# A chain of graph networks on one core: three root products and the first weight splits placed among the sort's permutation batches, the input loaded in five parts

## The chip, the core and the metric

The kernel runs on one core of a Trainium2 chip. The time is the device time of one execution in microseconds (us). The engines are named as in the profile: PE is TensorE, DVE VectorE, ACT ScalarE, POOL GpSimd, SP SyncE. PEld is PE's weight load, which overlaps the matrix products. Every engine has a sequencer of its own that works its instructions off in program order and tells the others of progress through semaphores.

## The reference

The input is x with 625 nodes of 768 features and a list of 10,000 edges (src, dst, one of four types). Four graph networks follow on one another, each with a residual and a layer norm: a relational network of three layers, a two-layer graph convolution, and two attention networks. Only the first layer of the first one matters here:

```python
def _rgcn_conv(x, weight, root, bias, src, dst, etype):
    n = x.shape[0]
    out = x @ root + bias
    for r in range(NUM_REL):
        sel = etype == r
        self_f = sel.astype(x.dtype)
        deg = jnp.zeros((n,), x.dtype).at[dst].add(self_f)
        norm = jnp.where(sel, 1.0 / jnp.maximum(deg[dst], 1.0), 0.0)
        h_r = x @ weight[r]
        msgs = h_r[src] * norm[:, None]
        out = out + jax.ops.segment_sum(msgs, dst, num_segments=n)
    return out
```

## The kernel before

The graph is turned into four dense 625 x 625 matrices of edge counts, one for each relation, so that all sums over edges become matrix products. Building them is the first tenth of the program and the only part that the change touches. It has these steps.

**Front.** SP loads the edges (L749), then x as one transfer (`x_nat`, L750), the bias (L751) and the first five weight chunks (L758). DVE and POOL work out from the edges a place for each of them in an order by source and destination block.

**Sort.** Ten batches of 1,000 edges each. For a batch DVE makes one-hot matrices (`fill`, L1585 to L1593, four instructions, two buffers), and PE multiplies them (`permute`, L2475, eight products of 176 columns that all add into PSUM bank 0). Operand elements of these products lie eight fp16 elements apart (`[:, :, c]` with `BATCH` = 8). Among the batches x is transposed, one block of 125 nodes at a time: PE transposes (`turn`, six instructions, L2399), ACT rounds the result to `xT_hi` (L1021), DVE makes the remainder `xT_lo` (`lower`, L1532). The transposes use banks 5, 6 and 7 in turn. Weights are split in the same way: ACT makes `w_hi` (L1076), DVE `w_lo` (`weights`, L1656).

**Sweeps.** Three sweeps of 44 tiles. A tile holds 128 sorted edges. DVE makes a one-hot of the destination for each tile (L1632), and in the first two sweeps one of the source (L1630; ACT makes 27 of these 88, L1087 and L1092). PE adds their product into the banks (`tile_sums`, L2550): one product of 512 columns and one of 114, whose place in PSUM is worked out from a register at run time. Ten destination one-hots fit in the ring `onehot_dst`, so DVE may be ten tiles ahead. After a sweep ACT reads the banks.

**Root products.** x @ root is computed as ten pieces (two halves of the columns times five node blocks; `early`, L2499 to L2505). A piece is 18 products of 384 columns, accumulated in bank 7; ACT copies it out (L1057). Two of the pieces also load registers for the tiles to come. All ten stand in the sweeps: four after tiles 8, 17, 26 and 35 of the first, three after tiles 14, 24 and 34 of the second, one after tile 12 of the third and one after each of the first two sweeps.

The order is written out once, in `adjacency_plan`; PE, ACT and DVE each walk this list and take the steps that are theirs:

```python
for b in range(BATCHES):
    out += [("fill", b), ("perms", b)]
    if 0 <= b - 2 < NB:
        out.append(("turn", b - 2))
    if 0 <= b - 4 < NB:
        out.append(("lower", b - 4))
out += [("weights", 0, RAW), ("sorted",)]
```

SP loads a further weight chunk only when DVE has made `w_lo` of the chunk five before it. The functions, as the profile numbers their lines:

## Time and profile before

| | |
|---|---|
| median of 3 runs | 1485.93 us (1485.71 to 1486.21) |
| the profiled execution's own time | 1481.86 us |
| its span, first to last instruction | 1480.0 us |
| PE busy | 1385.7 us, 94% of the span |
| DVE, ACT, POOL busy | 53%, 29%, 37% |
| mean granted PE clock | 0.972 |

Times within the profile count from the first instruction. "Granted clock" is the share of 2.4 GHz that PE was given; it has two levels, 1.2 and 2.4 GHz (0.50 and 1.00). Where the profile holds no record of it the column reads 1.00. A product's duration in the profile includes the time until its result has left the array, so products in a row overlap; the distance from start to start is what one costs. "Idle before" names who ended an engine's wait; "issue" means that no semaphore of another engine did.

### The profile page before, as it was taken

Reading aid. Unit: us, or ns where it says so; the run is one execution under the profiler, and the core shown is the slowest. Engines: PE = TensorE matmul, PEld = TensorE weight load, DVE = VectorE, ACT = ScalarE, POOL = GpSimd, SP = SyncE. Lnnn points to the kernel's source line nnn. Section 1 sums busy time; section 2 is a strip of 40 time slices with the busy share of each in tenths; the row PEclk is TensorE's granted clock in tenths of the full one; section 3 lists DMA queues with packets and bytes.
Section 4 is the critical chain, followed back from the end, with each engine's and each line's share of the span. In section 5 each row is a group of like instructions: output and inputs, shape, how many; then the busy total and the mean of one; then the engine's idle time right before and its main releaser. Section 6 shows DMA issues by size and latency. Waiting matters only on the chain.

```text
span 1480.0 us, 22384 instructions
## 1 busy us (share of the span) xinstructions
PE 1385.7 (94%) x7674; PEld 1285.4 (87%) x7674; DVE 779.1 (53%) x1856; ACT 433.8 (29%) x932; POOL 543.5 (37%) x617
## 2 busy tenths in 40 slices
PE   5999999999999999999999899889988999788797
PEld 3677999999999999999999889889978977677784
DVE  7876755134444365662223443545464614599644
ACT  2555421101100011110111221244574334445431
POOL 8001243242425344343433342044335545345530
PEclk9999999999999999999999999999999999967899
DMA  3111111122343152341212121122102211200001
GB/s 114 54 31 36 33 42 55 33 64 65 99 131 114 38 149 60 102 134 49 65 35 63 54 64 33 39 81 77 33 22 75 75 43 38 75 1 1 1 11 53
DMA packets 57781, 86.46 MB, mean 58 GB/s; under 512 B 6447, under 2 KB 54438, under 8 KB 57563
## 3 DMA queue, kind: packets, MB, share of 16 engines
q1 hardware_dynamic: 45184, 65.82, 15.1%
q10 hardware_dynamic: 12504, 19.36, 4.3%
q8 instruction: 63, 1.03, 0.3%
q14 instruction: 30, 0.25, 0.1%
HBM read 83.24 MB, written 1.92 MB: 58 GB/s over the span
## 4 chain that ended last, share of the span: by engine, by line
PE 76%; DVE 13%; ACT 3%; POOL 3%; issue 3%; DMA 2%; DVEq 0%; ACTq 0%; SPq 0%; POOLq 0%
PE psum L2410 13%; PE psum L2414 13%; PE psum L2413 13%; PE psum L2427 8%; PE psum L2430 8%; PE psum L2888 4%; PE psum L2550 3%; DVE max_scratch L2115 2%; PE psum L2475 2%; POOL w_lo L904 2%; PE psum L2789 1%; PE psum L2793 1%; PE psum L2794 1%; PE psum L2938 1%; PE psum L2399 1%
## 5 line engine op out<-in xcount | busy, mean ns | idle before, releaser
L2410 PE MATMUL psum<-w_lo,xT_hi 128*125 128x384 f32 (+5 forms) x1140 | 390.3, 342 | 7.1 <-DVE x_nat L1843 2.6
L2414 PE MATMUL psum<-w_hi,xT_hi 128*125 128x384 f32 (+5 forms) x1140 | 385.7, 338 | 0.0
L2413 PE MATMUL psum<-w_hi,xT_lo 128*125 128x384 f32 (+5 forms) x1140 | 385.6, 338 | 0.0
L891 POOL CAST w_hi<-w_raw 128x384 fp32r<-128x384 f32 x190 | 104.4, 549 | 590.0 <-PE psum L2414 483.2
L2410 PEld LDWEIGHTS psum<-w_lo,xT_hi 128*125 128x125 f32 (+1 forms) x1140 | 213.4, 187 | 10.5 <-POOL w_lo L904 3.4
L1685 DVE TENSOR_TENSOR h_lo<-psum,h_hi 125x384 fp32r<-125x384 f32 (+1 forms) x120 | 67.0, 558 | 286.2 <-ACT h_hi L1064 284.9
L1064 ACT ACTIVATE h_hi<-psum 125x384 fp32r<-125x384 f32 (+1 forms) x120 | 59.1, 492 | 532.1 <-PE psum L2414 527.7
L2413 PEld LDWEIGHTS psum<-w_hi,xT_lo 128*125 128x125 f32 (+1 forms) x1140 | 213.9, 188 | 0.4
L2414 PEld LDWEIGHTS psum<-w_hi,xT_hi 128*125 128x125 f32 (+1 forms) x1140 | 213.4, 187 | 0.0
L893 POOL TENSOR_TENSOR w_lo<-w_raw,w_hi 128x384 fp32r<-128x384 f32 x190 | 200.9, 1058 | 15.2
L2427 PE MATMUL psum<-h_lo,adjacency 125*125 125x384 f32 (+3 forms) x600 | 203.5, 339 | 2.1 <-issue 1.9
L2430 PE MATMUL psum<-h_hi,adjacency 125*125 125x384 f32 (+3 forms) x600 | 202.8, 338 | 0.0
L904 POOL TENSOR_TENSOR w_lo<-w_raw,w_hi 128x384 fp32r<-128x384 f32 x86 | 88.9, 1066 | 108.6 <-ACT w_hi L1248 108.6
L2427 PEld LDWEIGHTS psum<-h_lo,adjacency 125*125 125x125 f32 (+1 forms) x600 | 111.4, 186 | 3.3 <-issue 2.7
L2430 PEld LDWEIGHTS psum<-h_hi,adjacency 125*125 125x125 f32 (+1 forms) x600 | 111.7, 186 | 0.0
L2888 PE MATMUL psum<-features,score_tiles 125*125 125x257 f32 (+2 forms) x380 | 106.3, 430 | 0.0
L2888 PEld LDWEIGHTS psum<-features,score_tiles 125*125 125x125 f32 x380 | 69.8, 187 | 27.4
L1868 DVE CUSTOM_DVE_ANT_0 score_products<-score_w_raw,score_a_rows 128x384 f32<-128x384 f32 (+2 forms) x116 | 58.1, 545 | 11.4 <-DMA score_w_raw<-weights_dram 7.9
L1829 DVE SCALAR_TENSOR_TENSOR x_nat<-psum,inv_degrees,x_nat 125x384 f32<-125x384 f32 x100 | 54.3, 609 | 11.2 <-PE psum L2430 10.8
L2938 PE MATMUL psum<-features,more_tiles 125*125 125x97 f32 x240 | 40.9, 346 | 15.2 <-DVE more_tiles L2171 15.2
L2938 PEld LDWEIGHTS psum<-features,more_tiles 125*125 125x125 f32 x240 | 39.1, 259 | 18.2 <-issue 15.2
L1632 DVE TENSOR_SCALAR onehot_dst<-iota,dst_of_sweep 128x625 bf16<-128x625 f16 x132 | 46.5, 387 | 14.0 <-PE psum L2550 13.8
(342 smaller groups left out, 2209.8 us busy)
## 6 DMA issues: line engine op xcount, KB each, us to landing
w_raw<-weights_dram SPq DMA_DIRECT2D x296, 192.0 KB, 2.4
score_w_raw<-weights_dram ACTq DMA_DIRECT2D x58, 192.0 KB, 2.8
x_nat<-x_dram SPq DMA_DIRECT2D x1, 1875.0 KB
x_residual<-x_dram SPq DMA_DIRECT2D x1, 1875.0 KB
score_a_rows<-L_gnn_a_src_dram ACTq DMA_DIRECT2D x8, 192.0 KB, 3.5
score_a_rows<-L_gnn_a_dst_dram ACTq DMA_DIRECT2D x8, 192.0 KB, 4.8
out_dram<-x_residual SPq DMA_DIRECT2D x4, 375.0 KB
rgcn_bias<-rgcn_bias_dram SPq DMA_DIRECT2D x1, 1125.0 KB
```

Of the source, the lines that this page charges most:

```text
L891: nc.gpsimd.tensor_copy(mem.wh[:, slot, :], mem.raw[:, raw_slot, :]).then_inc(w_hi_ready, 1)
L893: nc.gpsimd.tensor_tensor(mem.wl[:, slot, :], mem.raw[:, raw_slot, :], mem.wh[:, slot, :].bitcast(F32), ALU.subtract).then_inc(w_lo_ready, 1)
L904: nc.gpsimd.tensor_tensor(mem.wl[:, c % WRING, :], mem.raw[:, c % RAW, :], mem.wh[:, c % WRING, :].bitcast(F32), ALU.subtract).then_inc(w_ ...
L1064: nc.scalar.activation(mem.hh[0:p, slot, 0:HW], bank(ring_bank(u), 0, HW, p), ACT.Copy).then_inc(h_hi_ready, 1)
L1685: nc.vector.tensor_tensor(o, p, h, ALU.subtract).then_inc(h_lo_ready, 1)
L2410: ins = nc.tensor.matmul(o, h, wl, start=(j == 0), stop=False, skip_group_check=True)
L2413: nc.tensor.matmul(o, l, wh, start=False, stop=False, skip_group_check=True)
L2414: ins = nc.tensor.matmul(o, h, wh, start=False, stop=stop and j == k - 1, skip_group_check=True)
L2427: ins = nc.tensor.matmul(o, a, mem.hl[0:p, slot, 0:width], start=(s == 0), stop=False, skip_group_check=True)
L2430: ins = nc.tensor.matmul(o, a, mem.hh[0:p, slot, 0:width], start=False, stop=(s == NB - 1), skip_group_check=True)
L2888: ins = nc.tensor.matmul(bank(q.out_bank(u), 0, width), p, feat_flat(q, k, a, a + width), start=(k == 0), stop=(k == NB - 1), skip_group_c ...
L2938: ins = nc.tensor.matmul(bank(Q2.out_bank(h), b * Q2.w, b * Q2.w + Q2.w), source_tile(Q2, h, k)[:, nodes(b)], feat_flat(Q2, k, h * Q2.w, h ...
```

## The change

The list becomes a fixed one. The transposes of blocks 0 and 1 stand ahead of the first batch, those of blocks 2, 3 and 4 after batches 1, 2 and 3; the remainders follow two batches earlier than before. They use banks 4, 5, 6 and 3 in turn. The first five chunks of weights are split in batches 2 and 3, the sixth in batch 4, chunks 6 to 9 on ACT from batch 5. The root pieces of blocks 0, 1 and 2 of the first half stand after batches 5, 7 and 8. The sweeps keep seven: after tiles 10 and 24 of the first, 14 and 30 of the second, 12 of the third, and one after each of the first two sweeps. x comes in five transfers, three from SP and two from ACT, and the bias is loaded after the first weight chunks.

```diff
-        ROOTS_AFTER = ((8, 17, 26, 35), (14, 24, 34), (12,))
+        ROOTS_AFTER = ((10, 24), (14, 30), (12,))
+        FIRST_TURNS = (4, 5, 6, 3)
...
-        WEIGHTS_AFTER = {(0, 4): (RAW, RAW + 1), (0, 27): (RAW + 1, WRING), (1, 10): (WRING, 12), (1, 25): (12, 15),
+        WEIGHTS_AFTER = {(0, 20): (RAW + 1, WRING), (0, 42): (WRING, 12), (1, 24): (12, 15),
                          (1, 40): (15, 16), (2, 27): (16, 2 * WRING)}
...
+            beside = {0: [("lower", 0)], 1: [("turn", 2), ("lower", 1)], 2: [("turn", 3), ("split", 0, RAW), ("lower", 2)],
+                      3: [("weights", 0, RAW), ("turn", 4), ("lower", 3)],
+                      4: [("split", RAW, RAW + 1), ("weights", RAW, RAW + 1), ("lower", 4)],
+                      5: [("root",) + roots.pop(0), ("split", RAW + 1, WRING)],
+                      7: [("root",) + roots.pop(0)], 8: [("root",) + roots.pop(0)]}
+            out += [("turn", 0), ("turn", 1)]
             for b in range(BATCHES):
-                out += [("fill", b), ("perms", b)]
-                if 0 <= b - 2 < NB:
-                    out.append(("turn", b - 2))
-                if 0 <= b - 4 < NB:
-                    out.append(("lower", b - 4))
-            out += [("weights", 0, RAW), ("sorted",)]
+                out += [("fill", b), ("perms", b)] + beside.get(b, [])
+            out.append(("sorted",))
...
-            sp.dma_start(mem.xn[0:BP, :, :], x.rearrange("(m p) d -> p m d", p=BP)).then_inc(x_loaded, 16)
...
+            for m in (0, 2, 4):
+                sp.dma_start(mem.xn[0:BP, m, :], x[m * BP:(m + 1) * BP, :]).then_inc(x_loaded[m], 16)
...
+            act.wait_ge(edges_loaded, 48)
+            for m in (1, 3):
+                act.dma_start(mem.xn[0:BP, m, :], x[m * BP:(m + 1) * BP, :]).then_inc(x_loaded[m], 16)
...
                 if step[0] == "turn":
-                    turn_hi(0, KC, mem.xh, ACT.Copy, step[1])
-                    if step[1] in (2, 4):
-                        first_split((step[1] - 2) // 2 * RAW, step[1] // 2 * RAW)
+                    turn_hi(0, KC, mem.xh, ACT.Copy, step[1], FIRST_TURNS)
+                elif step[0] == "split":
+                    first_split(*step[1:])
...
                 elif step[0] == "turn":
-                    if step[1] == 0:
-                        pe.wait_ge(x_loaded, 16)
-                    turn(KC, of(mem.xn), 0, step[1])
+                    pe.wait_ge(x_loaded[step[1]], 16)
+                    if step[1] == 1:
+                        pe.wait_ge(sizes_ready, 1)
+                    turn(KC, of(mem.xn), 0, step[1], FIRST_TURNS)
                 elif step[0] == "root":
-                    early(*step[1:], step[1:] in ((0, 1), (1, 1)))
+                    early(*step[1:], step[1:] in ((0, 3), (1, 1)))
```

## Rows read from the trace of the kernel before

**Rows 1.** Busy time by stretch (us), granted clock, DMA share

```profile
core 0: us, PE busy (x) PEld busy (x) DVE busy (x) ACT busy (x) POOL busy (x), PEclk, DMA share, GB/s
0.00:19.10 19.10, 2.88 (x23) 2.12 (x23) 11.75 (x37) 3.85 (x5) 16.27 (x45) 1.00 0.42 132
19.10:50.90 31.80, 31.73 (x110) 17.83 (x110) 25.68 (x52) 7.11 (x16) 16.06 (x30) 1.00 0.17 64
50.90:83.30 32.40, 31.79 (x166) 24.06 (x167) 28.10 (x109) 22.56 (x63) 0.00 (x0) 1.00 0.17 52
83.30:114.70 31.40, 30.63 (x170) 22.93 (x168) 24.76 (x79) 18.72 (x31) 0.00 (x0) 1.00 0.13 39
114.70:142.10 27.40, 24.55 (x133) 17.59 (x132) 18.42 (x51) 12.93 (x24) 2.22 (x2) 0.94 0.12 37
```

**Rows 2.** Chain that ended last, front and sort (start us, us, what)

```profile
18.14 0.95 DVE tile_onehot L1593 x2
19.13 7.83 PE psum L2475 x24
26.96 1.25 PE psum L2399 x6
28.21 2.52 PE psum L2475 x8
...
43.27 7.58 PE psum L2475 x24
```

**Rows 3.** Groups by form on PE: 26 to 48 us, then 340 to 360 us

```profile
L2475 PE MATMUL psum<-tile_onehot,slot_onehot 125*128 125x176 f16 x52 | 17.6, 497 | 0.0
L2399 PE MATMUL psum<-ident,x_nat 125*128 125x125 f32 x30 | 7.2, 411 | 0.0
...
L2399 PE MATMUL psum<-ident,x_nat 125*128 125x125 f32 x30 | 3.6, 272 | 0.4 <-DVE xT_lo L1530 0.4
```

**Rows 4.** Timeline of DVE, batches 4 to 6 and end of sort

```profile
34.53 0.53 DVE L1585 TENSOR_TENSOR same_tile<-iota_wide,tile_h 125x704 f16<-125x704 f16 x1 [0.81 <-PE psum L2475]
36.51 0.99 DVE L1532 TENSOR_TENSOR xT_lo<-psum,xT_hi 128x375 fp32r<-128x375 f32 x2
...
47.74 2.43 DVE L1656 TENSOR_TENSOR w_lo<-w_raw,w_hi 128x384 fp32r<-128x384 f32 x5
```

**Rows 5.** Timeline of ACT in the sort

```profile
35.16 1.11 ACT L1021 ACTIVATE xT_hi<-psum 128x375 fp32r<-128x375 f32 x2 [2.64 <-PE psum L2399]
36.16 2.17 ACT L1076 ACTIVATE w_hi<-w_raw 128x384 fp32r<-128x384 f32 x5
```

**Rows 6.** Timeline of PE: a root piece, tiles, a piece with register loads

```profile
58.94 0.42 PE L2499 MATMUL psum<-w_lo,xT_hi 128*125 128x384 f32 x1
...
62.17 2.63 PE L2550 MATMUL psum<-onehot_dst,onehot_src 128*125 128x512 bf16 x18
64.62 0.42 PE L2499 MATMUL psum<-w_lo,xT_hi 128*125 128x384 f32 x1
...
68.31 4.08 PE L2550 MATMUL psum<-onehot_dst,onehot_src 128*125 128x512 bf16 x17
```

**Rows 7.** Timeline of PEld (weight loads, two for each tile)

```profile
54.68 0.34 PEld L2550 LDWEIGHTS psum<-onehot_dst,onehot_src 128*125 128x125 bf16 x2 [0.20 <-issue]
55.21 0.34 PEld L2550 LDWEIGHTS psum<-onehot_dst,onehot_src 128*125 128x125 bf16 x2 [0.20 <-issue]
...
69.22 0.63 PEld L2550 LDWEIGHTS psum<-onehot_dst,onehot_src 128*125 128x125 bf16 x4 [0.18 <-issue]
70.04 0.26 PEld L2550 LDWEIGHTS psum<-onehot_dst,onehot_src 128*125 128x125 bf16 x2 [0.18 <-issue]
...
139.17 0.34 PEld L2550 LDWEIGHTS psum<-onehot_dst,onehot_src 128*125 128x125 bf16 x2 [0.20 <-issue]
139.70 0.34 PEld L2550 LDWEIGHTS psum<-onehot_dst,onehot_src 128*125 128x125 bf16 x2 [0.20 <-issue]
```

**Rows 8.** Waits by engine, 51 to 148 us (us in total, times, longest)

```profile
PEld psum L2550 <- issue: 15.2, 53, 1.5
DVE onehot_dst L1632 <- PE psum L2550: 13.8, 5, 4.9
```

**Rows 9.** Granted clock 0.50: stretches, and PE's timeline in the first

```profile
888.40:891.60 3.20, 3.20 (x12) 0.50 0.00 0
137.40:140.80 3.40, 3.40 (x14) 0.50 0.14 49
...
888.83 0.52 PE L2413 MATMUL psum<-w_hi,xT_lo 128*125 128x384 f32 x1
889.15 0.52 PE L2414 MATMUL psum<-w_hi,xT_hi 128*125 128x384 f32 x1
```

**Rows 10.** Timeline of SP's queue: issue of x

```profile
1.96 0.34 SPq L750 DMA_DIRECT2D x_nat<-x_dram  x1
```

More of the change, by code:

```diff
@@ L398, in program @@
         edges_loaded = sem("edges_loaded")
-        x_loaded = sem("x_loaded")
+        x_loaded = [sem(f"x_loaded{m}") for m in range(NB)]
         bias_loaded = sem("bias_loaded")
@@ L749, in _ @@
                 sp.dma_start(mem.edges_i[0:BP, i, :], v.rearrange("(p t) -> p t", t=ET)).then_inc(edges_loaded, 16)
-            sp.dma_start(mem.xn[0:BP, :, :], x.rearrange("(m p) d -> p m d", p=BP)).then_inc(x_loaded, 16)
-            sp.dma_start(mem.bias0[0:BP, :, :].rearrange("p l d -> p (l d)"),
-                         rgcn_bias.rearrange("(a l) d -> a (l d)", a=1).to_broadcast([BP, RLAYERS * D])
-                         ).then_inc(bias_loaded, 16)
+            for m in (0, 2, 4):
+                sp.dma_start(mem.xn[0:BP, m, :], x[m * BP:(m + 1) * BP, :]).then_inc(x_loaded[m], 16)
             def load(c, slot, first=False):
@@ L762, in _ @@
                 load(c, c, first=True)
+            sp.dma_start(mem.bias0[0:BP, :, :].rearrange("p l d -> p (l d)"),
+                         rgcn_bias.rearrange("(a l) d -> a (l d)", a=1).to_broadcast([BP, RLAYERS * D])
+                         ).then_inc(bias_loaded, 16)
             with sp.Fori(1, XRES_AT // RAW) as i:
@@ L1669, in _ @@
                 elif step[0] == "lower":
-                    turn_lo(0, KC, mem.xh, mem.xl, False, step[1])
+                    turn_lo(0, KC, mem.xh, mem.xl, False, step[1], FIRST_TURNS)
                 elif step[0] == "tile":
```

## The prediction, made before the result was known

> **What bounds the kernel now.** The page gives PE 94% of the span, so the first question is whether PE is limited by its array everywhere. The busy times by stretch [rows 1] split the touched part: front to 19.1 us, sort to 50.9, then three sweeps of 32.4, 31.4 and 27.4 us. The whole edit lives in these 142 us. PE does 2.9 us of work in the front and is "busy" for nearly all of the rest, but a busy share counts overlapping durations, so start-to-start distances decide.
>
> The chain of waits [rows 2] says that the front is DVE's (one-hots until 19.1) and the sort PE's: a batch of eight products takes 2.52 us, a block of transposes 1.25, and they follow without a gap. Ten batches and five blocks are 31.5 of the 31.7 us.
>
> Two things hide behind "PE". The first is the clock. The granted column reads 1.00 in the sort, yet six transposes take 1.25 us, with a duration of 411 ns each, where the same form later takes 272 [rows 3]. The first tiles after the sort start 0.53 us apart, exactly as at 139 us [rows 7], where the clock is recorded at 0.50 [rows 9]. So I read the sort and the first eight tiles as 1.2 GHz. Only after tile 8 does a tile cost 0.27: nine of them from 62.17 to 64.62 [rows 6].
>
> The second is PE's own instruction stream. After a plain root piece nine tiles take 2.45 us; after a piece that also loads registers, 68.31 onward, they take about 3.9 [rows 6], with 0.18 us gaps on PEld that nobody else ended [rows 7], 15.2 us of such gaps in all [rows 8]. Tile instructions work out addresses, and at 0.41 to 0.45 us a tile the sequencer is slower than the array. A plain root piece (18 products, 3.23 us) lets it run ahead, and the next nine tiles then go at the array's pace. A root piece in the sweeps thus costs 3.23 us and gives back about 1.5. The same pause lets DVE fill its ring; DVE waited 13.8 us for PE in the sweeps [rows 8].
>
> **The change, part by part.**
>
> *x in five transfers.* In the front x has from 1.96 us [rows 10] until 10.7 (end of PE's counting) to bring blocks 0 and 1. They are 0.77 MB; at the front's 132 GB/s [rows 1] that is 5.8 us, so they are there. Nothing on the chain waited for x before, so this is worth 0 by itself. The two issues on ACT stand ahead only of four clears needed at 50 us. The bias is needed after the sweeps: 0. The first weights are needed at about 30 us, behind 2.1 MB on SP's queue, or 16 us at that rate: 0.
>
> *Transposes 0 and 1 ahead of batch 0.* They lie in PE's idle time before 19.1: -2 x 1.25 = -2.5 us. If x were late they would delay batch 0 by as much as they miss; nothing in the rates says so.
>
> *Remainders and splits earlier, on DVE.* A fill takes about 2.0 us, a remainder 1.0, five w_lo 2.43 [rows 4]. Before, a batch with a transposition cost PE 3.77 and DVE 3.0, so DVE had 0.8 to spare, and the w_lo stood at the end beside batches 8 and 9, hidden. Now they stand in front of fill 4. I follow DVE: fill 0 ends 18.97, remainder 0, fill 1 ends 22.1, where PE was free at 21.6 (wait 0.5). Fills 2 and 3 are in time (29.4). Then DVE waits for ACT, whose five splits (2.17 us, [rows 5]) follow the rounding of block 3 and end at 32.5: w_lo done 33.1, remainder 3 at 34.1, fill 4 at 36.3. PE has finished batch 3 and transposition 4 at 33.4: wait 2.9. In the same way w_lo 5 and remainder 4 put fill 5 at 39.8 against 38.9: wait 0.9. Sum +4.3 us; bounds 0 (DVE catches up) and 4.3. I take 4.3.
>
> *Three root pieces into the sort.* PE has no gap there, so they lie on the path in full: 3.23 us each at the full clock, 18 x 0.32 = 5.76 at the slow one (889.15 - 888.83, [rows 9]), so 9.7 to 17.3 us. Dense products did raise the clock at 58.9, after the first tiles, while thirty microseconds of batches did not. So I expect each piece to begin slow and end fast and take the middle, 4.5 us: +13.5. ACT's copies and splits 6 to 9 run beside: 0.
>
> *What the batches after a root piece cost.* The trace has no batch at the full clock. Bounds: 2.52 us as now, or half, 1.26, for batches 6 to 9 (-5.0). A batch product takes 315 ns for 176 columns, where a plain product at the slow clock takes 320 for 384 [rows 2, 9]. It is limited by something other than the column rate, and I take it as unchanged: 0.
>
> The Trainium skill, "SBUF — State Buffer", section "Door 1: The DMA port swizzle", says that reads which enter a new 16-byte line each time pay a penalty. The operands here lie 16 bytes apart. The trace agrees that these products are slow (315 ns), not that the penalty ignores the clock. [...]
>
> *The sweeps without them.* Three plain pieces fewer: 3 x (3.23 - 1.5) = -5.2 us, plus one w_lo (0.5) that leaves DVE there: -5.7. Bounds: -9.7 if the tiles stay at 0.27 with no piece to run ahead in, and -4 if DVE, which needs 0.52 us for a tile with both one-hots, becomes the limit at the four w_lo now after tile 20. I take -5.7. The slow start of the sweeps stays: batch 9 and the wait for the sorted edges stand before it, as now.
>
> **Sum.** -2.5 + 4.3 + 13.5 = +15.3 in the sort (its end moves from 50.9 to about 66), -5.7 in the sweeps, net +9.6 us. On the profiled execution: 1481.86 + 9.6 = 1491.5. That one is 4.1 us below the median of the runs, so for the median I take 1485.93 + 9.6 = 1495.5 us.
>
> **Rivals.**
>
> *The clock rises and the batches follow it* (the other side). If the first root piece (5 us, starting slow) lifts the clock for good, pieces two and three take 3.23, and if batches scale with it, 6 to 9 take 1.26: sort +11.4 - 2.5 + 4.3 - 5.0 = +8.2. The sweeps then start at full clock and save the 1.2 us of bank starts too: -6.9. Net +1.3, 1487 us; if the tiles also kept 0.27, up to -3, 1483. It decides from the point where a batch takes under 1.6 us. For it: idle PE and slow clock vanish together. Against: 315 ns is not a column rate.
>
> *The clock stays up, the batches do not speed up.* Sort +11.4 + 1.8 = +13.2, sweeps -6.9: +6.3, 1492 us.
>
> *The slow clock holds throughout.* Each piece 5.76: sort +19.1, sweeps -5.7: +13.4, 1499 us.
>
> *The reorder does what it says.* PE's idle time in the sweeps is what the pieces leave, all 9.7 us come back, and DVE's waits in the sort do not appear: +13.5 - 2.5 - 9.7 = +1.3, 1487 us, and faster only with the cheaper batches (-3.7). Against: [rows 8] shows gaps that no root piece caused.
>
> **Numbers.** Forecast, slow-starting pieces with unchanged batches: 0.50. Clock up, batches unchanged: 0.14. Slow throughout: 0.10. Batches scale with the clock: 0.16, half of it within 3 us of before. Full return from the sweeps: 0.10. Range 1484 to 1500 us: from the scaling case with a little return, to slow throughout. The likeliest case's own range is 1491 to 1499. A measurement of this kernel tells about 0.2% (3 us) from no change. Slower: the first three, 0.74. The last two are split: same 0.14, faster 0.12.
>
> **What would show it.** Batch 0 still at 19.1 us, with twelve transposes before it. PE gaps before batches 1, 4 and 5. Root products 320 ns apart at the start of a piece and 176 at its end. Batches 6 to 9 at 2.52 us each. End of sort at 64 to 68. In the sweeps tiles at 0.44 after the pieces' lead is used up, and DVE's wait for PE well below 13.8 us. All after the sweeps is unchanged and shifted. The prediction is wrong above all if batches 6 to 9 are much shorter than 2.5 us, or if the three sweeps together lose over 9 us.

## The result, and the profile after

The changed kernel takes 1495.58 us (median of 4 runs, 1494.39 to 1496.47); the kernel before, run beside it, 1485.82 us (median of 4, 1483.34 to 1486.21). The ratio is 1.0065, 95% interval 1.0052 to 1.0079: slower by 9.8 us. 1495.5 was predicted.

The stretches of the changed kernel, and below them three shorter ones at one clock level. The sweeps are cut here where the bank products of each begin, some 3 us later than the inner cuts of [rows 1]:

```profile
core 0: us, PE busy (x) PEld busy (x) DVE busy (x) ACT busy (x) POOL busy (x), PEclk, DMA share, GB/s
0.00:19.10 19.10, 5.70 (x36) 4.30 (x36) 11.17 (x37) 5.79 (x9) 16.27 (x45) 1.00 0.44 136
19.10:64.90 45.80, 42.33 (x153) 27.50 (x153) 25.84 (x52) 8.51 (x19) 13.83 (x30) 0.96 0.18 61
64.90:97.00 32.10, 30.71 (x151) 21.17 (x151) 29.46 (x114) 24.45 (x68) 0.00 (x0) 0.89 0.13 38
97.00:127.20 30.20, 28.76 (x150) 20.00 (x151) 23.02 (x73) 16.18 (x24) 0.00 (x0) 1.00 0.09 27
127.20:152.00 24.80, 22.27 (x115) 15.08 (x116) 18.19 (x49) 9.87 (x18) 2.21 (x2) 0.86 0.14 41
46.70:51.50 4.80, 4.80 (x18) 2.26 (x17) 2.00 (x4) 2.14 (x5) 0.00 (x0) 1.00 0.00 0
65.70:72.50 6.80, 6.62 (x23) 3.58 (x22) 6.73 (x29) 4.94 (x16) 0.00 (x0) 0.50 0.01 2
144.20:151.00 6.80, 6.20 (x23) 3.78 (x24) 5.97 (x19) 0.00 (x0) 0.99 (x1) 0.50 0.22 68
```

The front is as long as before, and the sort lasts 45.8 us instead of 31.8. From bank products to bank products, the last to the product behind the last tile, the sweeps take 35.3, 31.3 and 24.1 us before and 32.0, 30.2 and 24.7 after. The last tile moves from 142.1 to 151.8 us, by 9.7, and the medians differ by 9.8: what happens until the last tile is the whole effect. (The two profiled executions differ by 14.2 us in their spans. The other 4.5 us lie behind the last tile, in work that the change does not touch, and are not in the medians.)

PE's timeline in the changed kernel. The transposes of block 1 waited for x, batches 1, 4 and 5 for DVE's one-hots, and the first root piece begins with products 0.32 us apart and ends with products 0.17 to 0.18 us apart:

```profile
10.51 1.49 PE L2406 MATMUL psum<-ident,x_nat 125*128 125x125 f32 x6
15.80 1.51 PE L2406 MATMUL psum<-ident,x_nat 125*128 125x125 f32 x6 [3.79 <-DMA x_nat<-x_dram]
19.09 2.74 PE L2482 MATMUL psum<-tile_onehot,slot_onehot 125*128 125x176 f16 x8 [1.78 <-DVE tile_onehot L1600]
22.18 2.74 PE L2482 MATMUL psum<-tile_onehot,slot_onehot 125*128 125x176 f16 x8 [0.35 <-DVE tile_onehot L1600]
...
36.27 2.74 PE L2482 MATMUL psum<-tile_onehot,slot_onehot 125*128 125x176 f16 x8 [2.56 <-DVE tile_onehot L1600]
39.56 2.74 PE L2482 MATMUL psum<-tile_onehot,slot_onehot 125*128 125x176 f16 x8 [0.55 <-DVE tile_onehot L1600]
41.86 0.77 PE L2506 MATMUL psum<-w_lo,xT_hi 128*125 128x384 f32 x1
42.42 0.53 PE L2511 MATMUL psum<-w_hi,xT_lo 128*125 128x384 f32 x1
42.74 0.53 PE L2512 MATMUL psum<-w_hi,xT_hi 128*125 128x384 f32 x1
...
46.31 0.34 PE L2511 MATMUL psum<-w_hi,xT_lo 128*125 128x384 f32 x1
46.49 0.33 PE L2512 MATMUL psum<-w_hi,xT_hi 128*125 128x384 f32 x1
...
46.67 5.27 PE L2482 MATMUL psum<-tile_onehot,slot_onehot 125*128 125x176 f16 x16
```

The last row is batches 6 and 7. They start at 46.67 and 49.23 us, 2.56 us apart, while the granted clock is 1.00 (the row 46.70:51.50 above): the higher clock gives a batch nothing. By starts, from batch to batch, the sort is now ten batches of 2.55 us, three blocks of transposes of 1.22, gaps of 0.54, 2.78 and 0.75 us before batches 1, 4 and 5, and pieces of 4.6, 4.7 and 3.2 us. A gap is some 0.2 us longer than the wait that the row shows.

DVE's timeline around the longest gap, with the wait for ACT's splits and the five `w_lo` ahead of fill 4:

```profile
28.89 0.51 DVE L1600 TENSOR_TENSOR tile_onehot<-same_tile,code_h 125x704 f16<-125x704 f16 x1
30.90 2.49 DVE L1663 TENSOR_TENSOR w_lo<-w_raw,w_hi 128x384 fp32r<-128x384 f32 x5 [1.50 <-ACT w_hi L1083]
33.32 0.99 DVE L1539 TENSOR_TENSOR xT_lo<-psum,xT_hi 128x375 fp32r<-128x375 f32 x2
34.23 0.51 DVE L1592 TENSOR_TENSOR same_tile<-iota_wide,tile_h 125x704 f16<-125x704 f16 x1
```

The waits after the sort (the totals of [rows 8]):

```profile
PEld psum L2557 <- issue: 19.5, 73, 1.6
DVE onehot_dst L1639 <- PE psum L2557: 10.1, 4, 3.4
```

With fewer pieces in the sweeps, PE's own instruction stream holds up the tiles 73 times instead of 53, 4.3 us more in all, and DVE waits 3.7 us less for room in its ring.

### The profile page after: what moved, and what is told of

The parts are those of the page before. It is cut to its first block, busy times and chain, and to the rows that moved or that the text cites. A ratio compares the mean times of both kernels' runs of the same rounds, so it can differ in the third digit from the quotient of the medians.

```text
span 1494.2 us, 22392 instructions
## 1 busy us (share of the span) xinstructions
PE 1398.4 (94%) x7674; PEld 1292.3 (86%) x7674; DVE 780.9 (52%) x1856; ACT 433.2 (29%) x932; POOL 540.9 (36%) x617
## 4 chain that ended last, share of the span: by engine, by line
PE 75%; DVE 14%; ACT 4%; POOL 3%; issue 2%; DMA 2%; DVEq 0%; ACTq 0%; SPq 0%; POOLq 0%
PE psum L2417 13%; PE psum L2421 13%; PE psum L2420 13%; PE psum L2434 8%; PE psum L2437 8%; PE psum L2896 5%; DVE max_scratch L2122 2%; PE psum L2946 2%; POOL w_lo L908 2%; PE psum L2557 1%; PE psum L2797 1%; PE psum L2801 1%; PE psum L2802 1%; PE psum L2482 1%; DVE onehot_dst L1639 1%
## 5 line engine op out<-in xcount | busy, mean ns | idle before, releaser
L1836 DVE SCALAR_TENSOR_TENSOR x_nat<-psum,inv_degrees,x_nat 125x384 f32<-125x384 f32 x100 | 54.3, 610 | 11.2 <-PE psum L2437 10.8
L2557 PE MATMUL psum<-onehot_dst,onehot_src 128*125 128x512 bf16 (+1 forms) x264 | 52.9, 336 | 4.2 <-DVE onehot_dst L1639 2.5
```

The lines of the kernel that those rows point to most:

```text
L2557: ins = nc.tensor.matmul(o, sources, mem.oh_dst[:, n % OH_RING, w:w + 512 if w == 0 else NC], start=False, stop=(t == GROUP - 1), skip_gro ...
```

## The experiments

The steps of the change were built up one by one, first on the kernel before (turns, splits), then with its root pieces moved elsewhere or cut. All stage times below are from one profiled execution of each; "last tile" is the start of PE's first product behind the last tile. Each ratio is against executions of the kernel before made beside that run (medians 1484.80 to 1486.12 us), so between rows made at different times the ratios are compared, not the medians.

| kernel | sort ends | last tile | against before | ratio, 95% interval |
|---|---|---|---|---|
| before | 50.7 | 142.1 | | |
| turns ahead | 49.5 | 140.2 | -1.9 | 0.9985 [0.9973, 0.9998] |
| and splits early | 52.3 | 143.5 | +1.4 | 1.0004 [0.9991, 1.0018] |
| and three pieces in the sort, cut short | 53.3 | 140.2 | -1.9 | 0.9988 [0.9977, 0.9999] |
| and these pieces whole: the change | 64.8 | 151.8 | +9.7 | 1.0065 [1.0052, 1.0079] |
| the change, its three pieces together | 64.9 | 151.5 | +9.4 | 1.0059 [1.0041, 1.0078] |

**Turns ahead alone.** x in five transfers and transposes 0 and 1 ahead of batch 0; splits, `w_lo` and root pieces as before.

```diff
+            beside = {0: [("lower", 0)], 1: [("turn", 2), ("lower", 1)], 2: [("turn", 3), ("lower", 2)],
+                      3: [("turn", 4), ("split", 0, RAW), ("lower", 3)], 4: [("split", RAW, WRING), ("lower", 4)]}
+            out += [("turn", 0), ("turn", 1)]
             for b in range(BATCHES):
...
             out += [("weights", 0, RAW), ("sorted",)]
```

> Of the change only the five transfers of x, the two transposed blocks ahead of batch 0 and the earlier remainders; weight splits and all ten root pieces stand as before the change. My theory: the two transpositions (1.25 us each) lie in PE's idle time before 19.1 us, one remainder ahead of fill 1 costs a wait of about 0.35 us, so the sort ends near 48.7 us instead of 50.9 and the time is 2.1 us below the kernel before. Rival: what is gained ahead of the sort is lost again in the sort or the sweeps, 0 us.

Measured: 1482.62 us, ratio 0.9985 [0.9973, 0.9998], 2.2 us less than the 1484.80 of the kernel before beside it. PE's timeline shows the one thing that was not as expected:

```profile
10.52 1.49 PE L2403 MATMUL psum<-ident,x_nat 125*128 125x125 f32 x6
16.16 1.51 PE L2403 MATMUL psum<-ident,x_nat 125*128 125x125 f32 x6 [4.15 <-DMA x_nat<-x_dram]
19.09 2.74 PE L2479 MATMUL psum<-tile_onehot,slot_onehot 125*128 125x176 f16 x8 [1.43 <-DVE tile_onehot L1597]
```

Block 1 of x, issued on ACT's queue, was there only at 16.2 us. It is still hidden, with 1.4 us to spare. The sort gets 1.2 us shorter: two turns of 1.22 fewer, and gaps of 0.54 and 0.73 before batches 1 and 5, where DVE comes late.

**Splits early as well.** The steps of the change on DVE and ACT, with the root pieces still in the sweeps.

```diff
-        WEIGHTS_AFTER = {(0, 4): (RAW, RAW + 1), (0, 27): (RAW + 1, WRING), (1, 10): (WRING, 12), (1, 25): (12, 15),
+        WEIGHTS_AFTER = {(0, 27): (RAW + 1, WRING), (1, 10): (WRING, 12), (1, 25): (12, 15),
...
-                      3: [("turn", 4), ("split", 0, RAW), ("lower", 3)], 4: [("split", RAW, WRING), ("lower", 4)]}
+                      3: [("weights", 0, RAW), ("turn", 4), ("lower", 3)],
+                      4: [("split", RAW, RAW + 1), ("weights", RAW, RAW + 1), ("lower", 4)],
+                      5: [("split", RAW + 1, WRING)]}
...
-            out += [("weights", 0, RAW), ("sorted",)]
+            out.append(("sorted",))
```

> The first experiment, and the weight splits moved into batches 2 to 5 as in the change; all ten root pieces stay in the sweeps. My theory: w_lo 0 to 5 ahead of fills 4 and 5 make PE wait 2.6 and 0.6 us, so the sort ends near 51.8 us, and one w_lo less in the sweeps gives back up to 0.5: 2.6 to 3.1 us above the first experiment, 0.5 to 1 us above the kernel before. Rival: DVE's spare time in the sort takes the splits up, same time as the first experiment.

Measured: 1486.24 us, ratio 1.0004 [0.9991, 1.0018], 3.6 us above turns ahead alone; the sort ends 2.8 us later and the last tile comes 3.3 us later. Batch 4 starts at 36.28 as in the changed kernel. DVE's waits are a cost of their own, and the two steps together are no gain.

**Three pieces left out, sweeps as in the change.** The kernel before with the three pieces cut to one product each, all after batch 9.

```diff
-        ROOTS_AFTER = ((8, 17, 26, 35), (14, 24, 34), (12,))
+        ROOTS_AFTER = ((10, 24), (14, 30), (12,))
...
-        WEIGHTS_AFTER = {(0, 4): (RAW, RAW + 1), (0, 27): (RAW + 1, WRING), (1, 10): (WRING, 12), (1, 25): (12, 15),
+        WEIGHTS_AFTER = {(0, 4): (RAW, RAW + 1), (0, 20): (RAW + 1, WRING), (0, 42): (WRING, 12), (1, 24): (12, 15),
...
-            out += [("weights", 0, RAW), ("sorted",)]
+            out += [("weights", 0, RAW)] + [("root",) + roots.pop(0) for _ in range(3)] + [("sorted",)]
...
-                for j in range(KC):
+                whole = f > 0 or m > 2
+                for j in range(KC if whole else 1):
...
```

> The sort of the kernel before, the sweeps of the changed one; the three root pieces that the change moves are cut to one product each (17 of 18 products of each left out), placed between the last batch and the sweeps, where the short copies make PE wait about 1 us. It prices what the sweeps give back without a root piece's work anywhere else. My theory: 1.4 to 1.9 us for each piece (the rest goes into the lost lead of PE's sequencer), so 4.1 to 5.7 us less, plus about 1: 3 to 4.7 us below the kernel before. Rival: each piece gives back its full 3.23 us: 9.7 - 1, so 8.7 us below.

Measured: 1486.99 us, ratio 1.001 [0.9998, 1.0023]. It does not answer the question: the first bank product comes at 59.6 us instead of 51.4. PE's timeline:

```profile
50.48 0.76 PE L2500 MATMUL psum<-w_lo,xT_hi 128*125 128x384 f32 x1
54.89 0.68 PE L2500 MATMUL psum<-w_lo,xT_hi 128*125 128x384 f32 x1 [3.64 <-ACT x_nat L1057]
56.15 0.68 PE L2500 MATMUL psum<-w_lo,xT_hi 128*125 128x384 f32 x1 [0.58 <-ACT x_nat L1057]
59.63 1.61 PE L2516 MATMUL psum<-init_columns,init_rows 2*125 2x512 bf16 x4 [2.80 <-issue]
```

The second product waits for ACT's copy of bank 7, and ACT, in its order, first splits weights 5 to 9, which arrive only after the `w_lo` at the end of the sort. By this order, pieces in the sort need the early splits too. The sweeps took 83.8 us here, but behind a pause of 9 us in which DVE filled its ring, so that figure is not the change's.

**The three pieces together, after batch 8.**

```diff
-                      5: [("root",) + roots.pop(0), ("split", RAW + 1, WRING)],
-                      7: [("root",) + roots.pop(0)], 8: [("root",) + roots.pop(0)]}
+                      5: [("split", RAW + 1, WRING)],
+                      8: [("root",) + roots.pop(0) for _ in range(3)]}
```

> The changed kernel with its three sort pieces one after the other behind batch 8 instead of behind batches 5, 7 and 8. My theory: the batches let the clock fall, so only the first piece starts at 1.2 GHz: 4.7 + 3.3 + 3.3 = 11.3 us instead of 4.8 + 5.0 + 3.4 = 13.2, so 1.9 us below the changed kernel. Rival: the pieces' place in the sort does not matter, same time as the changed kernel; or the copies of bank 7 between neighbouring pieces make PE wait 0.9 us twice, which eats the gain.

Measured: 1494.28 us, ratio 1.0059 [1.0041, 1.0078]; the sort ends at 64.9. PE's timeline at the seams between the pieces:

```profile
55.06 0.44 PE L2506 MATMUL psum<-w_lo,xT_hi 128*125 128x384 f32 x1 [0.58 <-ACT x_nat L1064]
59.06 0.44 PE L2506 MATMUL psum<-w_lo,xT_hi 128*125 128x384 f32 x1 [0.58 <-ACT x_nat L1064]
```

By starts, as above, the first piece takes 4.6 us from the end of batch 8 (49.7 to 54.3), the second and third 3.3 each (55.06 to 58.3, 59.06 to 62.3): one slow start, as expected. But the second and the third begin 0.7 us late, behind ACT's emptying of bank 7, and from the end of batch 8 to batch 9 it is 12.6 us, where the pieces apart took 12.5. Together or apart made no difference, since the clock's gain went to a new wait.

**The pieces in place, cut short.** The changed kernel with pieces 0 to 2 reduced to one product each (17 of 18 left out), nothing moved.

```diff
-                for j in range(KC):
+                whole = f > 0 or m > 2
+                for j in range(KC if whole else 1):
...
```

> The changed kernel with its three sort pieces cut to one product each (17 of 18 products of each left out), where they stand. Against the second experiment it has the same sort but seven instead of ten whole pieces in the sweeps, so it prices what the sweeps give back; against the changed kernel it prices the three pieces in the sort. My theory: sort ends near 53.3 us, sweeps take 86 to 87 us from their first bank start to the last tile where the second experiment takes 90.5, so 3 to 4 us below the second experiment and about 12 us below the changed kernel. Rival: the sweeps give back 9.7 us. Rival: the pieces cost the sort less than 9.7 us.

Measured: 1484.01 us, ratio 0.9988 [0.9977, 0.9999]. Its sweeps and those of the kernel with turns and splits only, which has all ten pieces there (first fence the cut one):

```profile
53.40:85.80 32.40, 30.87 (x151) 21.30 (x150) 29.43 (x114) 24.43 (x68) 0.00 (x0) 1.00 0.12 38
85.80:115.90 30.10, 28.65 (x150) 20.05 (x149) 23.06 (x73) 16.09 (x25) 0.00 (x0) 1.00 0.09 27
115.90:140.20 24.30, 21.60 (x115) 14.68 (x114) 18.21 (x49) 9.97 (x18) 2.22 (x2) 0.93 0.13 41
```

```profile
53.00:88.00 35.00, 34.91 (x185) 27.03 (x186) 28.52 (x110) 23.33 (x65) 0.00 (x0) 1.00 0.08 24
88.00:119.40 31.40, 30.66 (x169) 22.85 (x168) 23.76 (x74) 18.89 (x32) 0.00 (x0) 1.00 0.13 39
119.40:143.50 24.10, 21.29 (x115) 14.56 (x114) 18.01 (x49) 9.65 (x17) 2.22 (x2) 0.93 0.14 43
```

This is the accounting. The 51 products put back cost 11.5 us of sort (53.3 to 64.8) and almost nothing in the sweeps (86.9 us with them, 86.8 without). Three pieces taken out of the sweeps give back 90.5 - 86.8 = 3.7 us, though they hold 3 x 3.23 = 9.7 us of PE work: the first sweep gets 2.6 us shorter for two of them, the second 1.3 for one.

The split by sweep needs care, because the two kernels differ in one more thing. As in the change, two `w_lo` (0.5 us of DVE each) that stood after tile 10 of the second sweep stand after tile 42 of the first. No run moves them alone. But the kernel with evenly spread root pieces below has two pieces in the second sweep and these `w_lo` as before, and its second sweep takes 31.2 us, not 30.1. So some 1.1 of the 1.3 us seem to go with the two `w_lo`, and 0.1 with the piece. The total of 3.7 holds for pieces and `w_lo` together, and the first sweep's 2.6 carries the scatter of up to 1 us that "No piece in the third sweep" shows.

**Three transpositions ahead.** From turns ahead alone; block 2 is transposed in the front too, and the remainders are made later.

```diff
+            beside = {0: [("lower", 0)], 1: [("turn", 3), ("lower", 1)], 2: [("turn", 4)], 3: [("split", 0, RAW)],
+                      4: [("split", RAW, WRING), ("lower", 2)], 5: [("lower", 3)], 6: [("lower", 4)]}
+            out += [("turn", 0), ("turn", 1), ("turn", 2)]
...
```

> The first experiment with a third transposed block ahead of batch 0 (banks 4, 5, 6, 7, 3, 1, 2) and remainders 2 to 4 beside batches 4 to 6. My theory: PE is idle until 19.1 us and block 2 lands before 17, so another 1.25 us leaves the path: sort ends near 48.3 us, time 1.2 us below the first experiment and 3.4 below the kernel before. Rival: bank 1 is free only at 17.3 us, block 2 ends after 19.1 and delays batch 0, gain 0.

Measured: 1483.95 us, ratio 0.9993 [0.998, 1.0006]. The sort ends at 47.9 and the last tile comes at 138.4, 3.7 us before that of the kernel before, but the medians show less, and the interval's lower end (-3.0 us) does not reach it. The part after the last tile, the same in both programs, took 1341.3 us in this profiled execution and 1337.9 before. What sets this part's length was not tried; it stays open.

**Root pieces spread evenly.** The same, with pieces 4, 2 and 2 in the sweeps instead of 4, 3 and 1 (two more stand between sweeps in both), and the last four `w_lo` after tile 36 of the third sweep instead of 27.

```diff
-        ROOTS_AFTER = ((8, 17, 26, 35), (14, 24, 34), (12,))
+        ROOTS_AFTER = ((8, 17, 26, 35), (14, 28), (14, 28))
...
-                         (1, 40): (15, 16), (2, 27): (16, 2 * WRING)}
+                         (1, 40): (15, 16), (2, 36): (16, 2 * WRING)}
```

> The previous kernel with the root pieces of the later sweeps respread: after tiles 14 and 28 of the second and 14 and 28 of the third sweep (before: 14, 24, 34 and 12), and the last four w_lo after tile 36 instead of 27. My theory: in the third sweep PE idles 3.7 us behind DVE's w_lo and waits on its own sequencer, a piece there fills it and gives the sequencer a lead: 2 us below the previous kernel, 5 to 6 below the kernel before. Rival: DVE bounds the third sweep and PE's pieces only move, 0.

Measured: 1482.82 us, ratio 0.9982 [0.9971, 0.9993]; the last tile at 139.9, 1.4 us after that of three transpositions ahead (0.7 of it in the first sweep, which has the same pieces in both). The second sweep takes 31.2 us with two pieces as with three (31.3), the third 25.0 with two and 24.1 with one. So the spread gains nothing; taken out of the second sweep a piece saved 0.1, put into the third, together with the later `w_lo`, it cost 0.8.

**No piece in the third sweep.** The opposite, 4, 4 and 0.

```diff
-        ROOTS_AFTER = ((8, 17, 26, 35), (14, 24, 34), (12,))
+        ROOTS_AFTER = ((8, 17, 26, 35), (12, 22, 30, 38), ())
```

> The kernel with three transpositions ahead and the splits and root pieces as before, but with the one root piece of the third sweep moved into the second (4, 4, 0 instead of 4, 3, 1). Taking one out of the second sweep there cost nothing and adding one to the third cost 0.8 us, so if a piece is free in the second sweep because other work fills the same time, the last tile comes 0.8 us earlier than with 4, 3, 1 (138.4 to 137.6) and the kernel is 3.5 to 4.5 us faster than before at that point. Rival: a piece in the second sweep costs 1.1 us like the one taken out by the change, and the last tile moves by +0.3.

Measured: 1481.81 us, ratio 0.9974 [0.996, 0.9988], the fastest of the study, 3.9 us faster than before. Its last tile comes at 139.1, 0.6 us later than with 4, 3, 1, and neither expectation fits: a fourth piece is not free in the second sweep but lengthens it by 2.2 us (33.5), the third gets 2.7 us shorter (21.4), and the first, with the same pieces, took 1.2 us longer in this execution. What a piece costs in a sweep is thus no constant (0.1 us for the third of the second sweep, 2.2 for the fourth, whose neighbours moved too), and the 2.7 us of the third sweep are not the piece's alone: the granted clock is 1.00 in all of it here (117.69:139.00), while with 4, 3, 1 it is 0.50 from 132.7 to 136.1 us.

The 1.2 us of the first sweep come mostly from the clock. It rises during the first nine tiles or just behind them, earlier or later from one execution to the next. With 4, 3, 1 (first row) and with 4, 4, 0 (second row):

```profile
51.37 4.02 PE L2554 MATMUL psum<-onehot_dst,onehot_src 128*125 128x512 bf16 x18
51.35 5.05 PE L2554 MATMUL psum<-onehot_dst,onehot_src 128*125 128x512 bf16 x18
```

The kernel before lies between them with 4.93 us for the same nine tiles, turns ahead with 4.16. So a difference of up to 1 us in the first sweep of two profiled executions says nothing about their edits.

The intervals of the three kernels with three transpositions ahead overlap, and their order among each other is not settled.

**Products side by side.** The question left by batches 6 and 7: what holds a batch at 2.55 us at either clock.

```diff
+                if b in (3, 7):
+                    flat = mem.goal[0:BP, b % 2, :, :, :].rearrange("p k w c -> p (k w c)")
+                    own = mem.perm[0:BP, b % 2, :, :].rearrange("p w c -> p (w c)")
+                    for c in range(BATCH):
+                        nc.tensor.matmul(bank(1, 0, 2 * BLOCK_TILES, 128), mem.perm[0:BP, b % 2, :, c],
+                                         flat[:, c * 2 * BLOCK_TILES:(c + 1) * 2 * BLOCK_TILES],
...
+                    for c in range(BATCH):
+                        nc.tensor.matmul(bank(2, 0, 2 * BLOCK_TILES, 128), own[:, c * 128:(c + 1) * 128],
+                                         flat[:, c * 2 * BLOCK_TILES:(c + 1) * 2 * BLOCK_TILES],
```

> The changed kernel with 16 more products in front of the eight of batches 3 and 7, in banks that nobody reads: eight (A) whose moving operand is 176 adjacent elements instead of 176 elements 16 bytes apart, with the same strided weights, then eight (B) whose weights are adjacent too. Nothing is left out. Batch 3 stands in the slow clock (a root product there would take 320 ns for 384 columns), batch 7 in the fast one. The strided product takes 315 ns at either. Theory 'stride of the moving operand': the distance of the A products falls to the column rate or to the weight load, whichever is longer, so about 150 ns (176 columns at 1.2 GHz are 147, a strided weight load 146) in batch 3 and the same 146 or less in batch 7, and B differs little from A in batch 3. Rival 'load and product take turns' (146 + 170 = 315): A stays near 290 ns in batch 3 and falls to about 220 in batch 7, and B is the one that drops most. Rival 'instruction stream': all stay at 315 ns.

Measured, in PE's timeline (L2485 is A, L2489 is B, L2493 the batch's own products):

```profile
29.72 1.38 PE L2485 MATMUL psum<-tile_onehot,slot_onehot 125*128 125x176 f16 x8
30.90 1.38 PE L2489 MATMUL psum<-tile_onehot,slot_onehot 125*128 125x176 f16 x8
32.07 2.72 PE L2493 MATMUL psum<-tile_onehot,slot_onehot 125*128 125x176 f16 x8
...
50.77 0.79 PE L2485 MATMUL psum<-tile_onehot,slot_onehot 125*128 125x176 f16 x8
51.39 0.77 PE L2489 MATMUL psum<-tile_onehot,slot_onehot 125*128 125x176 f16 x8
52.00 2.69 PE L2493 MATMUL psum<-tile_onehot,slot_onehot 125*128 125x176 f16 x8
```

Eight A products take 30.90 - 29.72 = 1.18 us in batch 3 and 51.39 - 50.77 = 0.62 in batch 7: 147 and 77 ns each, where 176 columns at one a cycle are 147 ns at 1.2 GHz and 73 at 2.4. (For batch 3 the trace holds no record of the clock, so its level is read from these products; for batch 7 the granted clock is 1.00.) B takes the same. The eight own products of a batch take 2.55 us in both places (32.07 to 34.61; 52.00 to 54.5, where the root piece follows). So it is the moving operand, read 16 bytes apart; the weights, stored in the same way, cost nothing that this shows. "Load and product take turns" and "instruction stream" are out.

**The same operand stored adjacent.** The changed kernel, and turns ahead alone, with the 8 columns of a batch outermost in `same` and `goal`.

```diff
-        self.goal = at("tile_onehot", [128, 2, 2, BLOCK_TILES, BATCH], FP16, ah + 29152)
-        self.same = at("same_tile", [128, 2, BLOCK_TILES, BATCH], FP16, ah + 34784)
+        self.goal = at("tile_onehot", [128, 2, BATCH, 2, BLOCK_TILES], FP16, ah + 29152)
+        self.same = at("same_tile", [128, 2, BATCH, BLOCK_TILES], FP16, ah + 34784)
...
+            def beside_width(t, b):
+                return t[0:BP, b * BATCH:(b + 1) * BATCH].unsqueeze(2).to_broadcast([BP, BATCH, BLOCK_TILES])
...
-                    ins = nc.vector.tensor_tensor(mem.goal[0:BP, r, k, :, :], same, over_width(data, b, BLOCK_TILES),
+                    ins = nc.vector.tensor_tensor(mem.goal[0:BP, r, :, k, :], same, beside_width(data, b),
...
-                                           mem.goal[0:BP, b % 2, :, :, c].rearrange("p k w -> p (k w)"),
+                                           mem.goal[0:BP, b % 2, c, :, :].rearrange("p k w -> p (k w)"),
```

> The changed kernel with one storage order changed: the moving operand of the permutation batches and the mask it is made from lie with the 8 columns of a batch outermost, so that the 176 elements of one product are adjacent. Nothing is left out. By the products measured side by side, a batch falls from 2.55 us to about 1.2 us in the slow clock and 0.6 in the fast one, 14 to 17 us of PE work in all. What then sets the sort's pace is DVE: nine fills at 2.3 us, five remainders at 1.0, 2.9 us for six w_lo and about 1 us of waiting for ACT after 19.1 us come to 50 us, and the last root piece adds 3 to 4.5. If DVE's instructions keep their durations in the new order, the sort ends at 52 to 56 us instead of 64.8 and the kernel is 9 to 12 us faster than the changed one, within 2 us of before. Rival: DVE's three tile instructions slow down (operand repeated in the innermost dimension); at 0.73 us each instead of 0.53 a fill takes 2.9 us, and half of the gain goes. Second rival: PE waits more, the clock falls back to slow for the root pieces, and they cost 5.7 us each instead of 4.5.

> The same storage order in the kernel with two transpositions ahead and the splits and root pieces as before. PE's part of the sort falls from 31 to about 16 us, so DVE sets the pace: nine fills at 2.3 and five remainders at 1.0 after 19.1 us end at 45 to 46, and the last batch 1.2 us later, instead of 49.5. The kernel is 2.5 to 3.5 us faster than the same kernel with the old order, and 4.5 to 6 us faster than before (1480 to 1481.5 us). If DVE's three tile instructions take 0.73 us each, the sort does not get shorter and the kernel stays at 2 us faster than before.

Measured: from the changed kernel, 1487.81 us, ratio 1.0015 [1.0002, 1.0027], by the ratios 7.4 us better than without it, last tile at 144.8 instead of 151.8. From turns ahead alone, 1489.34 us, ratio 1.0026 [1.0013, 1.0038], by the ratios 6.1 us worse than without it, last tile at 146.8 instead of 140.2: the sort ends at 53.9 us instead of 49.5, and behind it the `w_lo` at its end now delay the first bank product by another 1.6. DVE's timeline of the first, one fill:

```profile
20.94 0.87 DVE L1595 TENSOR_TENSOR same_tile<-iota,tile_h 125x704 f16<-125x704 f16 x1
21.74 0.88 DVE L1598 TENSOR_TENSOR slot_onehot<-iota_wide,slot_h 125x1024 f16<-125x1024 f16 x1
22.54 0.88 DVE L1604 TENSOR_TENSOR tile_onehot<-same_tile,key_h 125x704 f16<-125x704 f16 x1
23.34 0.95 DVE L1604 TENSOR_TENSOR tile_onehot<-same_tile,code_h 125x704 f16<-125x704 f16 x1
```

A batch fell as expected (1.2 us slow, 0.7 fast), and the first rival held, larger than its 0.73 us: the three tile instructions went from 0.51 to 0.88 us, a fill from 2.2 to 3.3 us where these rows stand and from 1.9 to 3.0 later in the sort. Now DVE sets the sort's pace. In the changed kernel the root pieces fill some of PE's new idle time, so it gains; without them PE only waits. The Trainium skill, "VectorE: DVE Perf Modes", section "Mode 2×_1P — pack two bf16 into one 32-bit read", gives two results a cycle only to 16-bit operands whose elements are adjacent. The trace agrees as far as it goes: 704 elements took 0.51 us with adjacent elements in all operands and 0.88 with one repeated in the innermost dimension.

**Adjacent for PE, scattered write on DVE.** DVE reads as before and writes `goal` 352 bytes apart; from the kernel with no piece in the third sweep.

```diff
-        self.goal = at("tile_onehot", [128, 2, 2, BLOCK_TILES, BATCH], FP16, ah + 29152)
+        self.goal = at("tile_onehot", [128, 2, BATCH, 2, BLOCK_TILES], FP16, ah + 29152)
...
-                    ins = nc.vector.tensor_tensor(mem.goal[0:BP, r, k, :, :], same, over_width(data, b, BLOCK_TILES),
+                    ins = nc.vector.tensor_tensor(mem.goal[0:BP, r, :, k, :].rearrange("p c w -> p w c"), same, over_width(data, b, BLOCK_TILES),
...
-                                           mem.goal[0:BP, b % 2, :, :, c].rearrange("p k w -> p (k w)"),
+                                           mem.goal[0:BP, b % 2, c, :, :].rearrange("p k w -> p (k w)"),
```

> The fastest kernel so far (three transpositions ahead, splits as before, root pieces 4, 4, 0) with the moving operand of the batches stored so that a product's 176 elements are adjacent, but with DVE reading as before and writing that operand 352 bytes apart. Nothing is left out. In the other way of doing it DVE read an operand repeated in the innermost dimension, and its instructions went from 0.51 us to 0.88 us. Theory 'only the repeated operand slows DVE': a fill stays at 2.3 us, the sort becomes DVE's and ends 2 to 3 us earlier (45 to 46 instead of 47.9), and the kernel is 2 to 3 us faster than the one without it. Rival 'any innermost stride that is not adjacent slows DVE': the two writes take 0.88 us each, a fill 3.0, and the sort ends 3 to 5 us later.

Measured: 1535.79 us, ratio 1.0342 [1.0319, 1.0365]. The rival had the right sign and a quarter of the size:

```profile
26.64 3.53 DVE L1597 TENSOR_TENSOR tile_onehot<-same_tile,key_h 125x704 f16<-125x704 f16 x1
29.78 3.72 DVE L1597 TENSOR_TENSOR tile_onehot<-same_tile,code_h 125x704 f16<-125x704 f16 x1
```

A write takes 3.5 to 3.7 us instead of 0.51, 5 ns an element, and the sort ends at 100 us. Of the three places where the stride can be paid for, the one the kernel already had (PE's read) is the cheapest as long as PE has little else to do in the sort.

## Why the prediction was right

The sum was +15.3 in the sort and -5.7 in the sweeps. Measured were +14.1 (its end from 50.7 to 64.8 us) and -4.4 from there to the last tile. The two misses, 1.2 us too much in one and 1.3 too much in the other, cancel; this much of the 0.1 us between forecast and result is luck.

- *x in five transfers, 0.* Right in price, wrong in timing. I had blocks 0 and 1 there by 10.7 us; block 1 was there at 15.8. ACT issues it only at 4.29 us, behind its wait for the edges. By then SP has issued blocks 0, 2 and 4 (1.95 to 2.72 us) and three weight chunks, and my 5.8 us divided two blocks by the mean rate as if nothing else were queued. No run shows what each of the two cost. 1.8 us more and batch 0 would have been late.
- *Transposes 0 and 1, -2.5.* Two times 1.22 by starts, -2.4. Batch 0 stayed at 19.1 us.
- *DVE's waits, 0.5 + 2.9 + 0.9 = +4.3.* The gaps are 0.54, 2.78 and 0.75, +4.1, each before the batch that was named. The experiment with turns alone shows the first and the last of them without any early split: part of the 4.1 belongs to the transposes, and splits early cost 2.8 of sort.
- *Three root pieces, 3 x 4.5 = +13.5.* 4.6, 4.7 and 3.2, +12.5. The sum took all three as half slow. The clock rose in the first piece as assumed and fell again in the second (products 0.32 us apart from 52.2 to 55.4), so two pieces are in part slow, but the third ran fast throughout. In the kernel with products side by side the second piece ran fast too (3.1 us, 54.55 to 57.68), so how many pieces are slow is not fixed by their places. Putting the products back into the cut pieces gives 11.5 us for 51 of 54 products, and with them together nothing is saved: the step is shown.
- *Batches after a piece, 0.* Shown: 2.56 us apart at a granted clock of 1.00. The largest rival (batches scale with the clock, -5.0) falls. The "SBUF — State Buffer" page of the Trainium skill, in "Door 1: The DMA port swizzle", has each access that crosses to a new 16-byte line pay a penalty. The trace agrees for the moving operand: 147 and 77 ns adjacent, 318 ns at 16 bytes. That note gives no size and does not mention the clock; that the batches stay as they are is what the trace shows, 318 ns at either level. For the weights at the same distance the runs show no penalty.
- *The sweeps, -5.7.* The mis-sized term. Three pieces were to give back 1.73 us each and gave 3.7 us together; their 9.7 us of products covered 2.0 us each, not the 1.5 that I read from [rows 6]. By sweep the change gives -3.3, -1.1 and +0.6; most of the -1.1 seems to belong to the two `w_lo` that left the second sweep, which the sum did not price (it had one `w_lo` leave the sweeps). The +0.6 is not a matter of pieces: the third sweep has one in the changed kernel as before, and takes 24.3 us in the kernels with cut pieces and with the pieces together, where slow clock is recorded for 3.4 us of it as before, while here it is 6.8 us (144.20:151.00). I had put the clock of the sweeps down as unchanged but for their start. Another 0.6 us came back unforeseen between the last batch and the first bank product, 0.7 us before and 0.1 after.

So the reorder pays 12.5 us in a part of the kernel where PE is never idle, and gets 3.7 back from a part where PE was held up by its own instructions and DVE, and where the same pieces had hidden it. How much of that belongs to the instruction stream and how much to DVE no run separates.

## What to carry to other kernels

Price a piece of work by what the stage around it loses when it leaves, not by its own length: 9.7 us of products left the sweeps and 3.7 us came back, while in the new place they cost in full. Before giving an engine work "beside" others, count its start-to-start distances there; a busy engine with no gap has no room, and transposes moved into a real gap (PE idle before batch 0) were the one part of the change that gained (2.2 us). And when a product's time is not its column count over the clock, look at the operand's stride first, but ask who will pay for the other layout.

## What the hardware showed that was not expected

- A product with 176 fp16 columns read 16 bytes apart takes 318 ns both in the batches at 1.2 GHz (before the first record of the clock; the level is read from neighbouring products) and at a granted clock of 1.00; with adjacent columns 147 and 77 ns. Weights read 16 bytes apart load without any visible loss, even at 77 ns a product.
- DVE's 704-element fp16 instruction takes 0.51 us; with one input repeated in the innermost dimension 0.88 us; with the output written 352 bytes apart 3.5 to 3.7 us.
- A 375 KB block of x issued on ACT's queue at 4.29 us in the front was there only at 15.8 us (issued at 4.63, there at 16.2 with turns ahead alone); PE waited 3.8 and 4.2 us for it.
- The clock fell back to 0.50 in the middle of the sort (52.0 us), right after two batches at 1.00 between which PE had no idle time. With 16 more products ahead of batch 3 and of batch 7 (the second of the two), in the one execution profiled, it stayed at 1.00 from 47.6 to 68.0 us. Why it fell is open.
